# Feed-forward in one program block with attention, its front made in the last attention turn

## The reference

```python
q = (x @ Wq.T)                      # 32 heads of 128, RoPE
k_r, c_kv = x @ Wkr.T, x @ Wdk.T    # latent keys and values, 8 kv heads
k_c, v = c_kv @ Wupk.T, c_kv @ Wupv.T
y = softmax(causal(q k^T / sqrt(128))) v @ Wo.T
W = dequant(w, s)                   # int4 pairs in int32, one scale per 64
h = silu(x1 @ W1.T) * (x1 @ W3.T)   # hidden 1376
out = LayerNorm(x1 + h @ W2.T)
```

## Time and profile before

| what | us |
|---|---|
| median of 3 runs | 2494.77 (2494.61 to 2494.83) |
| the profiled execution's own time | 2494.45 |
| its span | 2492.7 |
| last instruction of attention on PE ends | 2066.05 |
| first product of feed-forward starts | 2086.72 |
| PE unbroken from | 2184.23 |

### The profile page before, as it was taken

The page is one execution under the profiler, slowest core; times in us unless marked ns, Lnnn a source line. Parts: engine busy times, 40 slices in busy tenths (PEclk is TensorE's granted clock), DMA queues, the critical chain, the costliest instruction groups (busy, mean ns, idle before and its releaser), DMA issues. The chain is left out here.

```text
span 2492.7 us, 40422 instructions
## 1 busy us (share of the span) xinstructions
PE 2411.8 (97%) x12028; PEld 2000.1 (80%) x12028; DVE 1428.0 (57%) x3333; ACT 1599.5 (64%) x3213; POOL 571.7 (23%) x445
## 2 busy tenths in 40 slices
PE   8999999999999999999999999999999996899998
PEld 7887888788888888887888888888878875678886
DVE  4334656666666666666666666666666665852332
ACT  4224878777787878787777877787877772332211
POOL 3002313222231323132231313131322202300000
PEclk9999999999999999999999999999999998899999
DMA  7767423324242323233242423232332316520100
GB/s 268 272 218 270 127 94 110 114 96 156 72 148 80 133 90 121 93 109 121 90 156 82 141 76 134 95 115 93 109 124 87 120 38 190 150 80 34 50 34 17
DMA packets 110979, 293.38 MB, mean 118 GB/s; under 512 B 10832, under 2 KB 27728, under 8 KB 101648
## 3 DMA queue, kind: packets, MB, share of 16 engines
q1 hardware_dynamic: 110928, 292.73, 35.4%
HBM read 208.80 MB, written 88.08 MB: 119 GB/s over the span
## 5 line engine op out<-in xcount | busy, mean ns | idle before, releaser
L908 DVE TENSOR_TENSOR b_pt<-b_tps,b_pt 128x512 fp32r<-128x512 f32 (+3 forms) x768 | 427.5, 557 | 335.2 <-ACT b_pt L751 334.2
L736 ACT ACTIVATE b_sc<-b_sc,b_rinv 128x896 f32<-128x896 f32 (+7 forms) x512 | 397.4, 776 | 306.8 <-DVE b_rinv L898 301.6
L245 PE MATMUL b_sps<-b_kt,b_qs 128*128 128x512 f32 (+4 forms) x2304 | 501.4, 344 | 10.8 <-DMA b_kt<-k_d 10.8
L245 PE MATMUL b_ps<-b_pt,b_vt 128*128 128x512 f32 x1728 | 479.9, 404 | 2.5 <-DVE b_ys L919 2.5
L245 PEld LDWEIGHTS b_sps<-b_kt,b_qs 128*128 128x128 f32 x2304 | 403.7, 188 | 71.2 <-issue 16.1
L245 PE MATMUL b_ps<-b_xs,b_wq 128*128 128x512 f32 x1536 | 444.8, 409 | 15.8 <-DVE b_qf L872 13.2
L245 PE MATMUL b_ps<-b_wo,b_ot 128*128 128x512 f32 x1536 | 424.0, 406 | 1.8 <-DVE b_ys L919 0.6
L751 ACT ACTIVATE b_pt<-b_tps 128x512 fp32r<-128x512 f32 (+3 forms) x768 | 364.9, 475 | 64.1 <-PE b_tps L1050 63.4
L730 ACT ACTIVATE b_sc<-b_sc,b_nmax 128x896 f32<-128x896 f32 (+7 forms) x512 | 392.5, 767 | 1.0 <-DVE b_nmax L890 1.0
L890 DVE CUSTOM_DVE_ANT_0 b_sc<-b_sps,b_mask 128x896 f32<-128x896 f32 (+7 forms) x512 | 380.9, 744 | 0.0
L1050 PE MATMUL b_tps<-b_ident,b_sc 128*128 128x128 f32 x2304 | 374.9, 273 | 2.4 <-DVE b_pt L908 1.6
(11 more groups left out here) (133 smaller groups left out, 2322.7 us busy)
## 6 DMA issues: line engine op xcount, KB each, us to landing
b_xs<-xs_d SPq DMA_DIRECT2D x32, 2048.0 KB, 8.9
b_ys<-y_d SPq DMA_DIRECT2D x128, 256.0 KB, 2.6
y_d<-b_ys SPq DMA_DIRECT2D x128, 256.0 KB, 2.1
k_d<-a_ks SPq DMA_DIRECT2D x32, 512.0 KB, 4.2
v_d<-a_vs SPq DMA_DIRECT2D x32, 512.0 KB, 3.0
b_kt<-k_d SPq DMA_DIRECT2D x64, 256.0 KB, 4.5
b_vt<-v_d SPq DMA_DIRECT2D x16, 1024.0 KB, 4.8
b_wraw<-in_wqT SPq DMA_DIRECT2D x64, 256.0 KB, 2.7
```

The lines of the kernel that those rows point to most:

```text
L245: ins = nc.tensor.matmul(out, *every[n], start=(n == 0), stop=(n == len(every) - 1))
L736: nc.scalar.activation(sc[:, slot, 0:w], sc[:, slot, 0:w], ACT.Copy, scale=rinv[:, slot:slot + 1])\
L908: nc.vector.tensor_tensor(pt[:, u, LO, 0:nj, h * P:(h + 1) * P], tps[n % 2][:, 0:nj], pt[:, u, HI, 0:nj, h * P:(h + 1) * P], ALU.subtract) ...
```

## The change

The two functions become one, `layer`, with one program block, so the engines no longer meet between attention and feed-forward; the buffers of stage C get fixed places over buffers of attention that are free by then, and its PSUM tiles are those of attention. Each old name of stage C gets the prefix `c_`.

A third plan, `FINAL`, serves the last turn. In it the four `q0` places, 12 matmuls each, are `ct` jobs of 4 (one transposed tile of the first sum block), at steps 22, 24, 26 and 29; as they are shorter, `wo` 3 and 4 and `pv` 4 and 5 come up to one step earlier, and steps 30 and 31 have no fill. In the last turn SP loads y of block 0 and weight tile 0 at step 17, DVE makes the statistics at steps 18 and 19, the scaling at 21 and 22 and unpacks tile 0 at 23 and 25, each behind the step's own jobs; ACT makes the square root at step 20 and the high parts at 24 and 26. In "end" DVE unpacks tiles 1 and 2 (steps 1, 3, 5, 7), and PE makes the first `up` at step 3. The later tiles are unpacked three items ahead (`EARLY`), not two; SP issues their loads, from tile 3 on, behind all of "end", the store of x1 and the wait for the last stores of y.

Besides: `unpack_down` uses two tensor-by-tensor shifts of 512 columns, the amounts read as a broadcast, for the four; norm2 has buffers of its own; in stage A the low part of the third late array moves from POOL to DVE, between `a_c_lo(0)` and `a_rope(0)`; in the first turn `va` 5 comes ahead of `q1` 0.

```diff
-FILL_FIRST = [('va', 3, 0, 0), ('va', 4, 0, 0), ('q1', 0, 0, 2), ('va', 5, 0, 3), ('va', 6, 0, 5),
+FILL_FIRST = [('va', 3, 0, 0), ('va', 4, 0, 0), ('va', 5, 0, 2), ('q1', 0, 0, 4), ('va', 6, 0, 5),
               ('va', 7, 0, 6)] + FILL[6:]
+TILE_AT = (22, 23, 24, 25)
+FILL_LAST = [('ct', f[1], 0, TILE_AT[f[1]]) if f[0] == 'q0' else f for f in FILL]
...
-    return 3 * (a + 1) if kind == "pv" else 12
+    return 3 * (a + 1) if kind == "pv" else 4 if kind == "ct" else 12
...
+FINAL = Plan(FILL_LAST, ROOM)
 DONE_AT = LOOP.done_at
 
 
 def plan_of(turn):
-    return FIRST if turn == "first" else LOOP
+    return FIRST if turn == "first" else FINAL if turn == "last" else LOOP
...
-    attention(nc, x, xT, wqT, wkrT, wdkT, wupkT, wupvT, woT, cosT, sinT, xs_d, k_d, v_d, y_d)
-    stage_c(nc, w13p, s13p, w2p, s2p, shifts, y_d, x1_d, out)
+    layer(nc, x, xT, wqT, wkrT, wdkT, wupkT, wupvT, woT, w13p, s13p, w2p, s2p, cosT, sinT, shifts,
+          xs_d, k_d, v_d, y_d, x1_d, out)
...
+        EARLY = 3
...
+                    if turn == "last" and step == 17:
+                        sp.wait_ge(add_done, 8 * GROUPS + ADD0)
+                        c_load_y(0)
+                        sp.wait_ge(s_done, CELLS * LAST + 16)
+                        c_weights(0)
+                    if turn == "end" and step == 0:
+                        sp.wait_ge(s_done, CELLS * GROUPS)
+                        c_weights(1)
+                    if turn == "end" and step == 4:
+                        c_weights(2)
...
+            c_store_x1(0)
             for p in range(2):
                 sp.wait_ge(y_out[p], 16 * 4 * GROUPS + YO0)
+            for f in range(EARLY, FT):
+                c_weights(f)
+                if f == EARLY:
+                    c_next_y(1)
+            c_store_x1(1)
...
-            for n in range(len(LATE)):
-                a_weight_lo(n)
+            a_weight_lo(0)
+            a_weight_lo(1)
...
+            for f in range(FT):
+                for m in range(3):
+                    pool.wait_ge(c_w_hi, 3 * f + m + 1)
+                    lo, src = split_views(m, f, LO)
+                    nc.gpsimd.tensor_tensor(lo, src, split_views(m, f, HI)[0], ALU.subtract).then_inc(c_w_lo, 1)
...
+            def c_tile_hi(t, ps):
+                act.wait_ge(c_t_done, t + 1)
+                nc.scalar.activation(c_xs(0)[:, HI, :, t * P:(t + 1) * P], ps.rearrange("p (k t) -> p k t", k=DC),
+                                     ACT.Copy).then_inc(c_t_hi, 1)
...
+            def c_block_of(n, first, last):
+                for index, (kind, what) in enumerate(items(last)):
+                    if kind == "t":
+                        c_transposed_hi(n + 1, what)
+                        continue
+                    c_hidden(n, index, what)
+                    if first and what + EARLY < FT:
+                        c_weights_hi(what + EARLY)
...
+                    if turn == "last" and step == 20:
+                        norm1.square_root(act, 0)
+                    if turn == "last" and step in (24, 26):
+                        c_weights_hi(0, (0, 1) if step == 24 else (2,))
+                    if turn == "end" and step in (2, 4):
+                        c_weights_hi(1, (0, 1) if step == 2 else (2,))
+                    if turn == "end" and step in (6, 8):
+                        c_weights_hi(2, (0, 1) if step == 6 else (2,))
...
+                if type(t) is int and t == 0:
+                    dve.wait_ge(a_w_hi, 3)
+                    nc.vector.tensor_tensor(LATE[2][2](LO), LATE[2][1], LATE[2][2](HI), ALU.subtract)\
+                        .then_inc(a_wv1_lo, 1)
...
+            def c_unpack_down(f):
+                n, b = width(f), f % 2
+                v = c_pk[b][0:n, 2].rearrange("p (c m) -> p c m", c=4)
+                nc.vector.tensor_tensor(v, v, c_sh[0:n, 1:5, 0:1].broadcast_to((n, 4, P)), ALU.logical_shift_left)\
+                    .then_inc(c_shifted, 1)
+                dve.wait_ge(c_shifted, 4 * f + 3)
+                nc.vector.tensor_tensor(v, v, c_sh[0:n, 1:5, 1:2].broadcast_to((n, 4, P)), ALU.arith_shift_right)\
+                    .then_inc(c_shifted, 1)
+                dve.wait_ge(c_shifted, 4 * f + 4)
+                c_multiply(f, 2, n, D)
+            def c_tile_lo(t, ps):
+                dve.wait_ge(c_t_hi, t + 1)
+                nc.vector.tensor_tensor(c_xs(0)[:, LO, :, t * P:(t + 1) * P], ps.rearrange("p (k t) -> p k t", k=DC),
+                                        c_xs(0)[:, HI, :, t * P:(t + 1) * P], ALU.subtract).then_inc(c_x0_lo, 1)
...
+                    if first and what + EARLY < FT:
+                        c_unpack_up(what + EARLY)
+                        c_unpack_down(what + EARLY)
...
+                    if turn == "last" and step == 18:
+                        dve.wait_ge(c_y_in, 16)
+                        norm1.tile_statistics(0, (0, 1))
+                    if turn == "last" and step == 19:
+                        norm1.tile_statistics(0, (2, 3))
+                        norm1.variance(dve, 0)
+                    if turn == "last" and step == 21:
+                        norm1.reciprocal_root(dve, 0)
+                        norm1.scale_tiles((0, 1))
+                    if turn == "last" and step == 22:
+                        norm1.scale_tiles((2, 3))
+                    if turn == "last" and step == 23:
+                        dve.wait_ge(c_sh_in, 16)
+                        c_unpack_up(0)
+                    if turn == "last" and step == 25:
+                        c_unpack_down(0)
+                    if turn == "end" and step in (1, 5):
+                        c_unpack_up(1 + step // 5)
+                    if turn == "end" and step in (3, 7):
+                        c_unpack_down(1 + step // 7)
...
+            def c_first_tile(t, bk, a, b):
+                if a == 0:
+                    pe.wait_ge(norm1.done, t + 1)
+                for k in range(a, b):
+                    last = nc.tensor.transpose(bank[bk][:, k * P:(k + 1) * P], c_yb[:, t, k * P:(k + 1) * P], ident[:])
+                if b == products("ct", t):
+                    last.then_inc(c_t_done, 1)
...
+                    if turn == "end" and step == 3:
+                        pe.wait_ge(sc_done, CELLS * GROUPS + SC0)
+                        pe.wait_ge(c_x0_lo, 4)
+                        c_item(0, 0, "f", 0)
...
+            pe.wait_ge(pt_lo, PIECES * GROUPS + PTLO0)
+            pe.wait_ge(ot_lo, QT * GROUPS)
+            pe.wait_ge(y_added, QT * GROUPS)
+            with pe.Fori(0, END) as n:
+                c_block_of(n, False)
+            c_block_of(END, True)
```

More of the change, by code:

```diff
@@ L253, in attention, with layer @@
+def layer(nc, x, xT, wqT, wkrT, wdkT, wupkT, wupvT, woT, w13p, s13p, w2p, s2p, cosT, sinT, shifts,
+          xs_d, k_d, v_d, y_d, x1_d, out):
     with ExitStack() as ctx:
@@ new lines, in c_block_of @@
+            def c_block_of(n, first, last):
[6 more added lines that the diff above has]
+                        c_weights_hi(what + EARLY)
+                    if what == 0 and not first:
+                        norm2.square_root(act, n - 1)
+                    if what == 2 and not last:
+                        norm1.square_root(act, n + 1)
@@ new lines, in c_residual, with c_statistics2 @@
+            def c_residual(n):
+                dve.wait_ge(c_x1_in, 16 * n + 16)
+                for t in range(4):
+                    if t < 3:
+                        dve.wait_ge(c_y_done, 3 * n + t + 1)
+                    else:
+                        dve.wait_ge(c_h_used, FT * (n + 1) + HU0)
+                    nc.vector.tensor_tensor(norm2.tile(t), c_y[t], norm2.tile(t), ALU.add).then_inc(c_z_done, 1)
+            def c_statistics2(n):
+                dve.wait_ge(c_z_done, 4 * n + 4 + Z0)
+                nc.vector.memset(norm2.tmp[:], 0.0)
+                norm2.statistics(dve, n)
@@ new lines, in c_statistics1, with c_block_of @@
+            def c_statistics1(n):
+                dve.wait_ge(c_y_in, 16 * n + 16)
+                nc.vector.memset(norm1.tmp[:], 0.0)
+                norm1.statistics(dve, n)
+            def c_block_of(n, first, last):
+                for index, (kind, what) in enumerate(items(last)):
+                    if kind == "t":
+                        c_transposed_lo(n + 1, what)
+                        continue
+                    c_gate(n, index, what)
+                    if what == 0 and not first:
+                        c_residual(n - 1)
+                    c_hidden_lo(n, what)
+                    if first and what + EARLY < FT:
+                        c_unpack_up(what + EARLY)
+                        c_unpack_down(what + EARLY)
+                    if what == 0 and not first:
+                        c_statistics2(n - 1)
+                    if what == 1 and not first:
+                        norm2.normalise(dve, n - 1)
+                    if what == 2 and not last:
+                        c_statistics1(n + 1)
```

(26 more changed lines are left out.)

640 lines of the change are left out of this document (264 added, 376 removed).

## The result

The kernel after takes 2533.9 us (median of 4 runs, 2532.1 to 2537.8), the kernel before beside it 2494.7; the ratio is 1.016, interval 1.0148 to 1.0173. The prediction was 2472, faster. The profiled execution took 2532.07 for a span of 2530.0.

A forecast was written before the change was run, and what follows sets the result against it. PE, busy 97%, was taken as the bound, with the DVE and ACT ring close beside it; gains of 18.7 (last turn to `up` 9), 2.0 (start) and 2.4 (first turn), 23.1 off 2494.77, gave 2472 us, range 2457 to 2482.

The forecast's parts named there:

- The loop turns are out of the question, as nothing in them changes.: Attention loop: its turns were taken as unchanged, so no gain or loss was counted there.
- The front forecast at 18.7: From the last attention turn to `up` of tile 9 in block 0: that `up` starts 18.7 us earlier.
- end: Stage after the last turn: 72 PE matmuls without a gap in 16.8 us, no wait before `pv` 7.
- E: Slower rival: clock falls at step 18 of the last turn, PE becomes the bound until tile 9; 2520 us, chance 0.03.
- Sum for the last turn: Last attention turn: added DVE work, table loads and wait for y, less slack, make it 14.5 us later; bounds 3 and 19.
- Rival C: Clock falls in the last turn and stays down through "end" and part of block 0; 2482 us, chance 0.12.
- The table loads priced at 2.0: Last turn: ACT's square root between exponentials needs two table loads, 2.6 us less 0.6 hidden in idle time, 2.0.
- Tile 3: Block 0: DVE waits some 9 us for tile 3's late weights; its unpacking, 4.1, delays gate 1 to 2100.3.
- so that a round becomes 7.8: Block 0: the pair of two-tensor shifts takes 1.3 us, saving 1.8 of DVE's 9.6 us round per tile.
- Start: Stage A: moving a late low part from POOL to DVE shortens PE's wait before 47.65; gain 2.0 us, bounds -0.5 and 3.6.
- First turn: First attention turn: `va` 5 covers the wait of `q1` 0 for the second half of x; gain 2.4 us.
- What comes behind it is the same work: Behind `up` of tile 9 in block 0: the same work in both kernels, so no change was counted.

The follow-up runs named there:

- e1: The kernel after with DVE's loop of stage A whole again, its first block no longer written out: 2488.2 us, ratio 0.9972 to the kernel before.
- e15: e5 with SP's weight loads issued earlier, and ACT making a copy instead of the first sum block's square root (output wrong): 2472.6 us, ratio 0.9902.
- e5: e1 with DVE making the three low parts from weight tile 3 on, POOL silent in the first feed-forward block: 2476.9 us, ratio 0.992.

## Why the prediction was wrong

**The step that failed is "The loop turns are out of the question, as nothing in them changes."** No instruction of the loop changed, but its place in DVE's program did, and the diff moved it: `a_block_of(0)` written out ahead of the loop of stage A. That cost 44.9 us by the marks (the 41 in the expectations left out the last return); in e1, which differs from after only in how DVE's stage A is written, 45.7 come back. The range stood on sums about the stages that the diff names, and no rival held this. The Trainium skill (Runtime: NRT & Kernel Launch, "Instruction fetch mechanics") has the rule: code comes in blocks of 256 instructions of which two are held, and a taken branch to a place outside them must fetch first. The runs agree: 256 more instructions lengthen no turn, 30 lengthen each, and DVE stands 6.2 to 7.2 us at a return. DVE stood there before anyway, 4.0 on average over the 13 returns, for PE. After, it is 85.8 / 13 = 6.6, so 2.6 more; PE's lower clock behind its gap is the likely rest of the 3.45.

That is not all: e1, without this loss, takes 2488.2, and the range was 2457 to 2482. The front forecast at 18.7 gave nothing, and the steps below say where it went: 4.8 lost in the last turn, 2.7 up to gate 1, 11.7 from gate 1 to `up` 9 (76.9 for 63.5 + 1.7), and 0.4 gained in "end", together 18.8. The one rival on the slower side, E at 0.03, rested on the clock alone.

**"Sum for the last turn": 14.5 predicted, 19.3 measured** (from the last load of keys to the last transposes 117.1 before, 136.4 after, 136.4 in e1), just above the 19 beyond which the prediction called itself wrong in the main; with the 134.3 to 137.8 of the other runs it is 17 to 21. DVE's added work was right (13.4 for 13.3), and the wait for y was 0.58 for 0.9. Missing is PE's clock: behind its long gaps PE is slower (three matmuls in 1.62 below, in 0.85 at 2070.79), and is then itself late. DVE's waits around 2081 to 2086 are 3.6 longer than their neighbours, which this would explain. It is read from the rows; no run isolates it. From 2031 to 2112 a clock of 0.94 was granted (1.00 in the stretch of the earlier trace rows):

```profile
2031.00:2112.00 81.00, 65.31 (x332) 53.11 (x331) 51.46 (x117) 52.35 (x91) 5.13 (x4) 0.94 0.32 100
...
2078.17 1.62 PE L249 MATMUL b_ps<-b_wo,b_ot 128*128 128x512 f32 x3 [3.74 <-DVE b_ot L1205]
```

Rival C had the falling clock, but not its course: it did not stay down, and "end" ran at 5.60 for 24. The table loads priced at 2.0 stay unmeasured (e15).

**"end": right.** No gap, 72 matmuls in 16.6 by the rows above (predicted 16.8), `pv` 7 without a wait.

**Tile 3: the wait is right, the gate is late.** DVE waited 9.5 for its load, as forecast (some 9); gate 1 came 19.7 behind the end of y's last addition for 17.0, since the unpacking in front of it took 6.2 and not 4.1. That is the next step's error.

**"so that a round becomes 7.8": wrong**, 9.84, and with it the stretch from gate 1 to `up` 9. I read from the earlier trace rows that an operation with two tensor operands never exceeds 0.693 "also beside POOL". But in the kernel before 31 of those 33 operations did not lie beside POOL's; the shifts did, and took the delay. Only two lay there, the first started before POOL's and the second directly behind it, and then it was POOL that was late: its three low parts took 4.79, where three at 1.27 take 3.8:

```profile
2089.25 1.28 DVE L1452 TENSOR_TENSOR c_sl<-c_pk,c_sl 128x512 f32<-128x512 int32 x2
...
2089.71 4.79 POOL L1389 TENSOR_TENSOR c_w<-c_sl,c_w 128x512 fp32r<-128x512 f32 x3 [3.95 <-ACT c_w L1397]
```

The pair only changed who is hit. The Trainium skill (SBUF — State Buffer, "Who interferes with whom") states what e5 shows: a DVE instruction with two inputs in SBUF contends with a GpSimd one that reads SBUF. It calls the lock exclusive, one waiting for all of the other, and the rows agree. In the round above DVE's slow shift ends at 2155.49, POOL's second low part at 2156.64, DVE's multiply at 2157.19: each ends 1.15 or 0.55 behind the other's end, about its own work, so they take turns. The start shows the same at length, after:

```profile
27.68 4.62 POOL L785 TENSOR_TENSOR a_wupv<-a_later,a_wupv 128x2048 fp32r<-128x2048 f32 x1 [2.44 <-ACT a_wupv L859]
...
30.25 4.19 DVE L1152 TENSOR_TENSOR a_wupv_lo<-a_raw,a_wupv_hi 128x2048 fp32r<-128x2048 f32 x1 [6.69 <-ACT a_wupv_hi L859]
...
44.63 2.33 DVE L1110 TENSOR_TENSOR a_xs<-a_xraw,a_xs 128x2048 fp32r<-128x2048 f32 x1 [2.51 <-ACT a_xs L869]
```

POOL's subtraction came first and took its usual 4.62; DVE's ended 2.14 behind POOL's end, and one alone takes 2.33. So DVE stood for about the 2.05 that they overlap.

**Start: 3.3 for 4.4.** The wait at 47.65 fell from 3.92 to 0.93, better than forecast, and the clock held: 1.00 from 48 to 56 for 0.65. But the subtraction priced at 2.3 took 4.19, as shown, and PE had a new wait of 2.69 for DVE at 35.70. The matmul that started at 56.02 before starts at 54.99: 1.0 gained for 2.0. **First turn: right**, no wait at 239; the other 2.3 of the 3.3 came here, for 2.4.

**"What comes behind it is the same work": work yes, time no**, 4.4 less. A matmul of `up` took 394 to 397 ns on average behind `up` 9 and takes 389 to 391. Weights and sums lie elsewhere in memory now; whether that does it wasn't tried and stays open.

Without the loop's loss the change (e1) gives 7.6 by the medians. In its profiled execution it is 9.0: 5.2 up to the last turn, -0.5 from there to `up` 9 (250.8 for 250.3), 4.3 behind. So the moved front itself gave nothing until POOL's part was taken away (e5, 11 more).

## What to carry over

An edit ahead of a loop moves the loop's code. For a long loop body (337 records of DVE a turn here), compare its place in the program and the fetch queue's packets before and after: 12 instructions ahead of it were free here, 30 cost 1.8% of the time. Keeping the prologue rolled was the cure here, because it put the loop back where it had been. A duration "beside another engine" is evidence only if the rows show that the two overlapped. That an operation moved between others also costs through the clock of the engine that waits for it is what the last turn's rows suggest, and no run has tested it.

## Unexpected on the hardware

256 empty instructions (a semaphore raised) took 21.5 us on DVE, 84 ns each. Of a DVE and a POOL subtraction that both read SBUF, the one that came later stood until the other was done: a DVE one of 2048 columns took 4.19 for 2.33. A return that missed its code fetched five packets of some 8 KB, and DVE stood 6.2 to 7.2 us at it, 52 times in four runs.
